# A post-layernorm transformer layer on one core: the output products stand behind the third query-key product, the row maxima go through DRAM in nine transfers, and the prologue is interleaved

## The chip, the cores and the metric

One Trainium2 chip, one of its cores. The metric is device microseconds of one execution of the whole program, the median of three runs.

## The reference

Sixteen sequences of 512 tokens with 256 channels pass through one layer. `x` is float32, shape (16, 512, 256).

```python
qkv = x @ qkv_w + qkv_b                       # 16 heads of 16 channels
local = local_attention(q, k, v)              # each query sees the 128 keys before it
rq = x @ rq_w + rq_b                          # 4 latent heads of 16 channels
rkv = mean_over_8_tokens(x) @ rkv_w + rkv_b   # 64 latent tokens
remote = latent_attention(rq, rk, rv) @ rout_w + rout_b
gate = sigmoid(local @ gl_w + remote @ gr_w)
x = layernorm(x + (gate * local + (1 - gate) * remote) @ out_w + out_b)
h = gelu(ternary_linear(x, w_up))             # 1024 channels; weights become -1, 0, 1
x = layernorm(x + ternary_linear(h, w_down))  # each linear first divides by the row's rms
```

## The kernel before

All instructions are written by hand for each engine, with semaphores between them; no scheduler moves anything. A sequence `i` goes through three phases of steps. Phase **P** makes what the attention needs: the query and key products `QK` to `QK+3` (128 rows each), which are stored as sums of three bf16 parts, the latent attention (`LAT_RQ`, `LAT_RKV`, `LAT_SCORES`, `LAT_EXP`, `LAT_NORM`, `LAT_T`, `LAT_O`, `REMOTE`) and the value products `VALUES` to `VALUES+3`. Phase **A/S/PV** is the local attention: 22 steps `A` find the row maxima of the scores, 16 steps `S` make the transposed scores with the maximum subtracted inside the product (its two bf16 parts are two more rows, `MAXR` and `MAXR+1`, of the stacked queries `Qs`), and 16 steps `PV` weigh the values. Phase **F** is the rest of the layer: `GATE`, `OUT` and `OUT+1` (the output products), `NORM`, `NORM+1` (layernorm and rms), `XN_T`, `XN_HI`, `XN_LO` (transpose and split into two fp16 parts), `UP` to `UP+7` with the down products two steps behind, and `END`.

The first half of body `i` is the local attention of sequence `i` with the maxima of `i+1` between its steps (`order_of_attention`). The second half interleaves phase F of sequence `i` with phase P of sequence `i+2`; its order is the table `SECOND_HALF`, which TensorE, ScalarE, VectorE and GpSimd all walk from top to bottom, each doing its own share of every step. So the table sets the order on all four engines at once, and an engine that waits in one step holds up its share of all the steps below. Fourteen of the sixteen bodies have P steps in their second half. Before body 0 stands the prologue (`order_of_prologue`), which holds phase P of sequences 0 and 1 and the steps A of sequence 0.

A query-key block is split in place. `QK+c` leaves the product in a PSUM bank; ScalarE copies it to `parts[:, 0]` as bf16 (L767); step `SPLIT+2c` subtracts that part in the bank on TensorE (L1392) and ScalarE copies the rest to `parts[:, 1]` (L774); `SPLIT+2c+1` does it again for `parts[:, 2]`. Only after this third copy is the bank given back (`p_taken`, L778). There are four such banks, and phase P hands them out in turn, in the order in which its results stand in the program: a result takes the bank of the result four places before it.

```python
                        act.wait_ge(part2, count(s, 4, t))
                        act.sem_inc(p_taken[bank], 1)
```

Step `LAT_RKV` is one copy `rqT` and four copies `lat_bd` on ScalarE (L783, L790) and then two small operations on VectorE that wait for them (L1076). `LAT_SCORES` on TensorE (L1424) waits for `lat_bd` as well. On ScalarE the feed-forward starts with an ACT_TABLE_LOAD and the GELU (L883), of which the first frees the bank for `UP+2` on TensorE.

SyncE issues all the DMAs in one stream. `restack(i+2)` writes the parts to DRAM (three DMAs for queries, three for keys, each waiting for its parts) and reads them back as stacks `Qs` and `Ks` (six and six). `move_max(i+1)` copies the transposed maxima `nmax_pair` (128 partitions, 2 parts, 64 columns) into the two rows of `Qs`; it waits for `split_maxima` on VectorE, which stands at step `UP+1`. The first step S of a sequence waits for these transfers (L1514).

## Time and profile before

| | |
|---|---|
| median of three runs | 1172.93 us (1171.77 to 1175.84) |
| the profiled execution | 1171.74 us |
| its span, first to last instruction | 1170.0 us |
| TensorE matmul busy | 994.1 us, 85% of the span |
| VectorE, ScalarE, GpSimd busy | 823.3, 741.7, 628.1 us |
| mean granted TensorE clock | 0.96 of 2.4 GHz |

The span has a prologue of 98.0 us up to the first step S, then bodies of about 66.3 us each (the first steps S start at 98.0, 169.2, 235.6, 301.8, 368.2 us and so on), and the last two bodies, which have less beside them. The busy time of a matmul contains waiting in the pipeline, so where TensorE bounds is read from its idle times and what ended them, stage by stage.

### The profile page before, as it was taken

To read this page: it belongs to the slowest core of one execution; us is meant where nothing else is said; L and a number is where in the kernel's file an instruction comes from. 1 tells how busy PE (TensorE), PEld (TensorE's weight loads), DVE (VectorE), ACT (ScalarE), POOL (GpSimd) and SP (SyncE) were. 2 spreads that over 40 slices of the span, in tenths; PEclk is the share of its full clock that TensorE was granted. 3 is DMA by queue.
4 is the path that set the end of the run, shared out by engine and by line. 5 is a ranking of instruction groups with operands and counts; after the bars stand their busy time and mean duration, and the time that the engine had idled before them with its cause. 6 is when DMAs were issued, how large, how long until landed. Compare 5 with 4: busy or idle time off the path is not lost. (4 is left out here: it accounts for less than half of the span.)

```text
span 1170.0 us, 37047 instructions
## 1 busy us (share of the span) xinstructions
PE 994.1 (85%) x15432; PEld 634.8 (54%) x15432; DVE 823.3 (70%) x1781; ACT 741.7 (63%) x1189; POOL 628.1 (54%) x790
## 2 busy tenths in 40 slices
PE   6765999898989989888999889898989988884755
PEld 3444565565656555565656555565656555562433
DVE  4485777786868777686868778686867768684544
ACT  3523666767676676767676677767676676762544
POOL 6014455665746465664746466574745466572754
PEclk8896999999999999999999999999999999996887
DMA  5731331506152341516143240516143250601000
GB/s 192 199 103 57 109 92 48 152 24 182 40 154 66 100 120 48 137 40 181 40 127 93 86 133 28 157 40 180 40 128 92 68 135 10 176 21 38 1 19 19
DMA packets 58868, 107.46 MB, mean 92 GB/s; under 512 B 20518, under 2 KB 38726, under 8 KB 55622
## 3 DMA queue, kind: packets, MB, share of 16 engines
q1 hardware_dynamic: 58556, 105.08, 31.8%
q8 instruction: 122, 2.00, 0.7%
q14 instruction: 46, 0.38, 0.1%
q10 hardware_dynamic: 144, 0.00, 0.0%
HBM read 70.87 MB, written 33.55 MB: 89 GB/s over the span
## 5 line engine op out<-in xcount | busy, mean ns | idle before, releaser
L847 ACT ACTIVATE Pt<-scores 128x1024 f32<-128x1024 f32 (+1 forms) x256 | 229.6, 917 | 143.9 <-PE oacc L1552 82.0
L1125 DVE TENSOR_REDUCE nmax<-work 128x3 f32<-128x480 f32 x352 | 215.1, 633 | 31.5 <-PE work L1503 28.2
L701 POOL TENSOR_TENSOR h_lo<-hbuf,h_hi 128x512 f16<-128x512 f32 x128 | 148.1, 1157 | 139.8 <-DVE h_hi L1252 139.8
L671 POOL TENSOR_SCALAR_AFFINE_SELECT Pt<-Pt 128x512 f32<-128x512 f32 x256 | 164.2, 642 | 67.6 <-ACT Pt L847 67.2
L685 POOL TENSOR_TENSOR rs<-rs,power 128x6 f32<-128x6 f32 x32 | 42.4, 1325 | 247.5 <-DVE rs L1229 247.5
L1552 PE MATMUL oacc<-Pt,Vp 128*32 128x256 f32 (+1 forms) x2048 | 153.2, 360 | 15.2 <-POOL Pt L675 9.4
L1529 PE MATMUL scores<-Qs,Ks 100*32 100x160 bf16 (+4 forms) x4096 | 119.9, 230 | 46.9 <-DMA Qs<-nmax_pair 25.7
L1498 PE MATMUL work<-Ks,Qs 98*32 98x160 bf16 x4096 | 146.3, 236 | 14.5 <-DVE nmax L1125 10.5
L1252 DVE CAST h_hi<-hbuf 128x512 f16<-128x512 f32 x128 | 69.2, 540 | 100.3 <-ACT hbuf L883 99.8
L1529 PEld LDWEIGHTS scores<-Qs,Ks 100*32 100x32 bf16 x4096 | 82.4, 98 | 92.2 <-ACT Pt L847 51.0
L1382 PE MATMUL scores<-xT,wqk 128*128 128x512 f32 x256 | 123.3, 616 | 6.5 <-DMA xT<-x_t 6.5
L1565 PE MATMUL oacc<-wdn_t,h_hi 128*128 128x256 f16 x512 | 118.1, 273 | 9.8 <-POOL h_lo L701 9.8
L675 POOL TENSOR_SCALAR_AFFINE_SELECT Pt<-Pt 128x512 f32<-128x512 f32 x192 | 121.8, 635 | 0.0
L1565 PE MATMUL oacc<-wdn_t,h_lo 128*128 128x256 f16 x512 | 117.9, 273 | 0.0
L774 ACT ACTIVATE parts<-scores,bqk 128x512 bf16<-128x512 f32 x128 | 86.2, 685 | 49.6 <-PE scores L1392 47.3
L883 ACT ACTIVATE hbuf<-work 128x512 f32<-128x512 f32 x128 | 76.0, 594 | 60.9 <-PE work L1622 59.1
L1498 PEld LDWEIGHTS work<-Ks,Qs 98*32 98x32 bf16 x4096 | 90.6, 97 | 40.3 <-DVE nmax L1125 26.1
L1622 PE MATMUL work<-xnT,wup_t 128*128 128x512 f16 x384 | 99.5, 382 | 5.8 <-DVE h_sum L1258 5.5
L1503 PE MATMUL work<-mask_band,identb 128*32 128x192 bf16 (+1 forms) x1408 | 100.4, 248 | 0.8 <-issue 0.8
L1258 DVE TENSOR_TENSOR h_sum<-h_sum,work 128x512 f32<-128x512 f32 x112 | 76.4, 682 | 10.8 <-ACT work L890 10.5
L1382 PEld LDWEIGHTS scores<-xT,wqk 128*128 128x128 f32 x256 | 48.9, 196 | 57.7 <-issue 54.9
L767 ACT ACTIVATE parts<-scores,bqk 128x512 bf16<-128x512 f32 x64 | 43.7, 683 | 55.5 <-PE scores L1382 55.3
(175 smaller groups left out, 1878.5 us busy)
## 6 DMA issues: line engine op xcount, KB each, us to landing
parts_scratch<-parts SPq DMA_DIRECT2D x96, 256.0 KB, 5.1
Qs<-parts_scratch SPq DMA_DIRECT2D x96, 256.0 KB, 5.0
Ks<-parts_scratch SPq DMA_DIRECT2D x96, 256.0 KB, 5.0
xT<-x_t SPq DMA_DIRECT2D x16, 512.0 KB, 4.0
xres<-x SPq DMA_DIRECT2D x16, 512.0 KB, 4.8
y<-nat SPq DMA_DIRECT2D x16, 512.0 KB, 3.0
Qs<-nmax_pair SPq DMA_DIRECT2D x256, 2.0 KB, 1.8
nat<-up_t SPq DMA_DIRECT2D x1, 1024.0 KB, 6.0
```

The source lines that it names most:

```text
L671: ins = pool.affine_select(out=pt[:, :, 0:P], in_=pt[:, :, 0:P], compare_op=ALU.is_gt, fill=0.0, base=0, pattern=[[0, 4], [1, P]], channel ...
L675: ins = pool.affine_select(out=pt[:, :, P:2 * P], in_=pt[:, :, P:2 * P], compare_op=ALU.is_ge, fill=0.0, base=0, pattern=[[0, 4], [-1, P]] ...
L701: pool.tensor_tensor(h_lo[:, t % NR, :], hbuf[:, t % 2, :], h_hi[:, t % NR, :], ALU.subtract).then_inc(h_lo_ready, 1)
L847: nc.scalar.activation(Pt[:, u % NPT, :, 0:w], scores[:, slot, :, :].rearrange("p k (h q) -> p (k h) q", h=2)[:, :, 0:w], ACT.Exp, scale=S ...
L1125: nc.vector.tensor_reduce(nmax[:, first:first + n], work[:, slot, 0:n * BAND].rearrange("p (h c) -> p h c", h=n), X, ALU.max, negate=True) ...
L1382: mm = nc.tensor.matmul(p_bank(bank), wqk[:, t, c * P:(c + 1) * P], xT[:, t, :], start=(t == 0), stop=False, skip_group_check=True)
L1498: nc.tensor.matmul(work[g * GT:(g + 1) * GT, slot, i * BAND:(i + 1) * BAND], q[0:KA, h, at:at + GT], kk[0:KA, h * S + at:h * S + at + BAND ...
L1503: mm = nc.tensor.matmul(o[:, :, 0:NG + 1:NG, :], identb[:, g * GT:(g + 1) * GT], mask_band[:, :, :].unsqueeze(1).to_broadcast([P, n, 2, GT ...
L1529: mm = nc.tensor.matmul(scores[g * GT:(g + 1) * GT, slot, c // 2, (c % 2) * 2 * P + lo:(c % 2) * 2 * P + hi], kk[0:KB, key + lo:key + lo + ...
L1552: mm = nc.tensor.matmul(oacc[c * PVW:(c + 1) * PVW, hg % 2, j * P:j * P + w], Vp[:, s.par, j, h * VW:h * VW + PVW], Pt[:, v % NPT, c, 0:w] ...
L1565: mm = nc.tensor.matmul(oacc[:, b // 2, (b % 2) * D:(b % 2 + 1) * D], (h_hi, h_lo)[j][:, f % NR, b * P:(b + 1) * P], wdn_t[:, f, :], start ...
L1622: mm = nc.tensor.matmul(work[:, slot, :], wup_t[:, t, f * P:(f + 1) * P], xnT[:, part, t, :], start=(part == 0 and t == 0), stop=(part == ...
```

## The change

Three edits.

The table `SECOND_HALF`: `OUT` moves from behind `QK+3` and `SPLIT+3` to directly behind `SPLIT+2`, that is, behind the third product; `OUT+1` follows two subtractions later; `QK+3` comes after it. `NORM` and `NORM+1` now stand ahead of `LAT_RKV`, with `LAT_RQ` and one subtraction between them. `SPLIT+7` comes after `LAT_RKV`; `XN_T` and `XN_T+1` come ahead of `VALUES+1` and `LAT_SCORES`; `LAT_EXP` and `LAT_EXP+1` come after `XN_LO`. From `UP` on the table is as it was.

The maxima: eight DMAs write `nmax_pair` to a scratch tensor in DRAM, in the layout of the two rows; SyncE waits until they have landed; a ninth DMA reads both rows into `Qs`. Before, sixteen DMAs wrote the rows directly.

The prologue: all steps P of sequence 1 stand between the steps A of sequence 0, whereas before its first fourteen stood ahead of them; the sums of the weights' magnitudes (`SUMS`) move from ahead of the first step A to behind the fourteenth.

```diff
--- before.py
+++ after.py
@@ -75,10 +75,10 @@
 END = UP + FT
 SECOND_HALF = (
     ("F", GATE), ("P", QK), ("P", QK + 1), ("P", SPLIT), ("P", QK + 2), ("P", SPLIT + 1), ("P", SPLIT + 2),
-    ("P", QK + 3), ("P", SPLIT + 3), ("F", OUT), ("P", SPLIT + 4), ("P", SPLIT + 6), ("P", LAT_RQ), ("P", SPLIT + 5),
-    ("F", OUT + 1), ("P", SPLIT + 7), ("P", LAT_RKV), ("P", VALUES), ("P", LAT_SCORES), ("F", NORM),
-    ("F", NORM + 1), ("P", LAT_EXP), ("P", VALUES + 1), ("F", XN_T), ("F", XN_T + 1), ("F", XN_HI),
-    ("P", LAT_EXP + 1), ("F", XN_LO), ("P", VALUES + 2), ("F", UP), ("P", LAT_NORM), ("F", UP + 1),
+    ("F", OUT), ("P", SPLIT + 3), ("P", SPLIT + 4), ("F", OUT + 1), ("P", QK + 3), ("P", SPLIT + 5), ("F", NORM),
+    ("P", LAT_RQ), ("P", SPLIT + 6), ("F", NORM + 1), ("P", VALUES), ("P", LAT_RKV), ("P", SPLIT + 7),
+    ("F", XN_T), ("F", XN_T + 1), ("P", VALUES + 1), ("P", LAT_SCORES), ("F", XN_HI), ("F", XN_LO), ("P", LAT_EXP),
+    ("P", LAT_EXP + 1), ("P", VALUES + 2), ("F", UP), ("P", LAT_NORM), ("F", UP + 1),
     ("P", VALUES + 3), ("P", LAT_NORM + 1), ("F", UP + 2), ("F", UP + 3), ("P", LAT_T), ("P", LAT_T + 1),
     ("F", UP + 4), ("P", LAT_O), ("F", UP + 5), ("P", REMOTE), ("F", UP + 6), ("P", REMOTE + 1), ("F", UP + 7),
     ("F", END))
@@ -140,13 +140,15 @@
     order += [("P", 0, k) for k in (LAT_SCORES, LAT_EXP, LAT_EXP + 1, VALUES, VALUES + 1, LAT_NORM, LAT_NORM + 1,
                                     VALUES + 2, VALUES + 3)]
     order += [("P", 0, LAT_T), ("P", 0, LAT_T + 1), ("W", 0, CONSTANTS)]
-    order += [("P", 1, k) for k in split]
-    order += [("P", 0, LAT_O), ("P", 1, LAT_RQ), ("P", 1, LAT_RKV), ("W", 0, SUMS)]
-    between = {1: [("P", 0, REMOTE)], 3: [("P", 0, REMOTE + 1)], 5: [("P", 1, VALUES)], 7: [("P", 1, LAT_SCORES)],
-               9: [("P", 1, LAT_EXP)], 10: [("P", 1, LAT_EXP + 1)], 12: [("P", 1, VALUES + 1)],
-               13: [("P", 1, LAT_NORM), ("P", 1, LAT_NORM + 1)], 14: [("P", 1, VALUES + 2)],
-               16: [("P", 1, LAT_T), ("P", 1, LAT_T + 1)], 17: [("P", 1, VALUES + 3)], 18: [("P", 1, LAT_O)],
-               20: [("P", 1, REMOTE), ("P", 1, REMOTE + 1)]}
+    order.append(("P", 0, LAT_O))
+    after = {0: [(0, REMOTE), (1, QK)], 1: [(1, QK + 1), (1, SPLIT)], 2: [(0, REMOTE + 1)],
+             3: [(1, QK + 2), (1, SPLIT + 1), (1, SPLIT + 2)], 4: [(1, QK + 3), (1, SPLIT + 3)],
+             5: [(1, SPLIT + 4), (1, SPLIT + 6)], 6: [(1, SPLIT + 5), (1, LAT_RQ), (1, SPLIT + 7)], 7: [(1, LAT_RKV)],
+             8: [(1, VALUES)], 9: [(1, LAT_SCORES)], 11: [(1, LAT_EXP)], 12: [(1, LAT_EXP + 1), (1, VALUES + 1)],
+             14: [(1, LAT_NORM), (1, LAT_NORM + 1)], 15: [(1, VALUES + 2)], 17: [(1, LAT_T), (1, LAT_T + 1)],
+             18: [(1, VALUES + 3)], 19: [(1, LAT_O)], 21: [(1, REMOTE), (1, REMOTE + 1)]}
+    between = {v: [("P", i, k) for i, k in steps] for v, steps in after.items()}
+    between[13] = [("W", 0, SUMS)]
     for v in range(NM):
         order.append(("A", 0, v))
         order += between.get(v, [])
@@ -331,6 +333,7 @@
         scores = ctx.enter_context(nc.psum_tensor("scores", [P, 2, 2, 512], F32))
         oacc = ctx.enter_context(nc.psum_tensor("oacc", [P, 2, 512], F32))
 
+        nmax_dram = nc.dram_tensor("nmax_scratch", [2, H * S], BF16, kind="Internal").ap()
         parts_dram = nc.dram_tensor("parts_scratch", [3, 2, P, 2 * S], BF16, kind="Internal").ap()
 
 
@@ -376,6 +379,7 @@
         s_taken = [sem(f"s_taken{k}") for k in range(2)]
         nmax_vec = sem("nmax_vec")
         nmax_split = sem("nmax_split")
+        nmax_out = sem("nmax_out")
         nmax_in = [sem(f"nmax_in{k}") for k in range(2)]
         masked = sem("masked")
         pv_done = sem("pv_done")
@@ -535,14 +539,16 @@
             def move_max(s):
 
                 wait_alone(sp, nmax_split, count(s, 1, 0))
-                for j in range(2):
-                    row = Qs[s.par][MAXR + j:MAXR + j + 1, :, :].rearrange("a h n -> a (h n)").rearrange(
-                        "a (k r w) -> a k r w", k=2, w=P)
-                    for g in range(NG):
-                        quadrant = slice(g * GT, (g + 1) * GT)
-                        for k in range(2):
-                            sp.dma_start(row[:, k, :, quadrant], nmax_pair[quadrant, j, k * GT:(k + 1) * GT]
-                                         ).then_inc(nmax_in[s.par], 16)
+                if not s.first:
+                    wait_alone(sp, nmax_in[1 - s.par], (s.half + s.par) * 16)
+                scratch = nmax_dram.rearrange("j (k r g w) -> g r j k w", k=2, g=NG, w=GT)
+                for g in range(NG):
+                    for j in range(2):
+                        sp.dma_start(scratch[g, :, j], nmax_pair[g * GT:(g + 1) * GT, j, :].rearrange(
+                            "p (k w) -> p k w", k=2)).then_inc(nmax_out, 16)
+                wait_alone(sp, nmax_out, count(s, 1, 0) * 16 * 2 * NG)
+                sp.dma_start(Qs[s.par][MAXR:MAXR + 2, :, :].rearrange("j h n -> j (h n)"), nmax_dram
+                             ).then_inc(nmax_in[s.par], 16)
 
             def store_before(s):
 
@@ -1132,7 +1138,7 @@
                     slot, k = work_use(s, "A", v)
                     dve.wait_ge(w_taken[slot], k + 1)
                 if not s.first:
-                    dve.wait_ge(nmax_in[1 - s.par], (s.half + s.par) * 16 * 4 * NG)
+                    dve.wait_ge(nmax_out, count(s, 1, -1) * 16 * 2 * NG)
                 nc.vector.transpose(nmaxT[:, :], nmax[:, :]).then_inc(nmax_vec, 1)
                 dve.wait_ge(nmax_vec, count(s, 2, 0))
                 nc.vector.tensor_copy(nmax_pair[:, 0, :], nmaxT[:, :]).then_inc(nmax_vec, 1)
@@ -1511,7 +1517,7 @@
                 hg, j = u // NB, u % NB
                 slot, k = score_use(s, u)
                 if u == 0:
-                    pe.wait_ge(nmax_in[s.par], (s.half + 1) * 16 * 4 * NG)
+                    pe.wait_ge(nmax_in[s.par], (s.half + 1) * 16)
                     if s.first:
                         pe.wait_ge(q_consts, 2)
                 if u < 2 and not s.last:
```

The table sets the order on every engine, so its effect is shown as the program of each engine has it. In these rows `scores<-xT,wqk` is a query-key product, `scores<-parts,minusb` a subtraction, `work<-wout,mixT` an output product, `scores<-wv,xT` a value product, `scores<-lat_bd,rqT` the latent scores, `oacc<-ident,mixT` the transposes of `XN_T`, and `oacc<-xnT,minus` the product of `XN_LO`.

TensorE, second half of a body, from the third query-key product on, before:

```order
L1382 MATMUL scores<-xT,wqk 128x512 x2
L1392 MATMUL scores<-parts,minusb 128x512
L1581 MATMUL work<-wout,mixT 128x256 x4
L1584 MATMUL work<-bout_rows,ones_b 128x256 x2
L1392 MATMUL scores<-parts,minusb 128x512 x2
L1399 MATMUL scores<-xT,wrq 64x256 x4
L1392 MATMUL scores<-parts,minusb 128x512
L1581 MATMUL work<-wout,mixT 128x256 x4
L1584 MATMUL work<-bout_rows,ones_b 128x256 x2
L1392 MATMUL scores<-parts,minusb 128x512
L1409 MATMUL scores<-pooled,wrk 64x64 x4
L1413 MATMUL scores<-wrv,pooled 64x64 x4
```

and after:

```order
L1587 MATMUL work<-wout,mixT 128x256 x4
L1590 MATMUL work<-bout_rows,ones_b 128x256 x2
L1398 MATMUL scores<-parts,minusb 128x512 x2
L1587 MATMUL work<-wout,mixT 128x256 x4
L1590 MATMUL work<-bout_rows,ones_b 128x256 x2
L1388 MATMUL scores<-xT,wqk 128x512 x2
L1398 MATMUL scores<-parts,minusb 128x512
L1405 MATMUL scores<-xT,wrq 64x256 x4
L1398 MATMUL scores<-parts,minusb 128x512
L1370 MATMUL scores<-wv,xT 128x272 x2
L1415 MATMUL scores<-pooled,wrk 64x64 x4
L1419 MATMUL scores<-wrv,pooled 64x64 x4
```

The first output product moved ahead of the fourth query-key product, and the latent keys and values moved behind the first value product.

TensorE a little further down, after the change, with the semaphores that it waits for:

```order
L1597 MATMUL oacc<-ident,mixT 128x128
L1597 MATMUL oacc<-ident,mixT 128x128 [waits xn_ready]
L1597 MATMUL oacc<-ident,mixT 128x128
L1370 MATMUL scores<-wv,xT0 128x272 [waits p_taken3]
L1370 MATMUL scores<-wv,xT0 128x272
L1430 MATMUL scores<-lat_bd,rqT 128x256 [waits p_taken0,p_taken1,bd_ready]
L1430 MATMUL scores<-lat_bd,rqT 128x256 x3
```

The second value product now stands behind the transposes and ahead of the latent scores; before, it stood behind the latent scores. Its bank is that of the fourth query-key product (`p_taken3`), where before it was that of the latent keys and values.

ScalarE, second half, from the third query-key copy on (`parts<-scores,bqk` are the copies of the split, `mixT<-ytok,nbias,rs` those of `NORM`, `Vp<-scores` those of the values), before:

```order
L767 ACTIVATE parts<-scores,bqk 128x512
L774 ACTIVATE parts<-scores,bqk 128x512 x5
L783 ACTIVATE rqT<-scores,brq 128x256
L790 ACTIVATE lat_bd<-scores,lat_fold 128x64 x4
L806 ACTIVATE Vp<-scores 128x16x17
L864 ACTIVATE mixT<-ytok,nbias,rs 128x256 x4
L799 ACTIVATE Pt<-Pt 128x512
L806 ACTIVATE Vp<-scores 128x16x17
L870 ACTIVATE xnT<-oacc 128x512 x2
L799 ACTIVATE Pt<-Pt 128x512
L874 ACTIVATE xnT<-oacc 128x512 x2
L806 ACTIVATE Vp<-scores 128x16x17
```

and after:

```order
L773 ACTIVATE parts<-scores,bqk 128x512
L780 ACTIVATE parts<-scores,bqk 128x512
L870 ACTIVATE mixT<-ytok,nbias,rs 128x256 x2
L780 ACTIVATE parts<-scores,bqk 128x512
L870 ACTIVATE mixT<-ytok,nbias,rs 128x256 x2
L812 ACTIVATE Vp<-scores 128x16x17
L789 ACTIVATE rqT<-scores,brq 128x256
L796 ACTIVATE lat_bd<-scores,lat_fold 128x64 x4
L780 ACTIVATE parts<-scores,bqk 128x512
L812 ACTIVATE Vp<-scores 128x16x17
L876 ACTIVATE xnT<-oacc 128x512 x2
L880 ACTIVATE xnT<-oacc 128x512 x2
```

The last copy of the split moved from ahead of `rqT` and `lat_bd` to behind them, and the exponentials of the latent scores (`Pt<-Pt`) moved behind the copies of `XN_HI` and `XN_LO`.

TensorE in the prologue, behind the gate's bias, after the change (`work<-Ks,Qs` is a step A of sequence 0; before, the first of them stood behind all the query-key products and subtractions of sequence 1):

```order
L1673 MATMUL oacc<-gcol,bog 128x1 x2
L1466 MATMUL scores<-Pt,rv_bd 32x256 x4
L1504 MATMUL work<-Ks,Qs 32x160 x12
L1509 MATMUL work<-mask_band,identb 32x3x2x32 x4
L1476 MATMUL scores<-lat_oT,wro 128x256 x4
L1388 MATMUL scores<-xT,wqk 128x512 x2
L1504 MATMUL work<-Ks,Qs 32x160 x12
L1509 MATMUL work<-mask_band,identb 32x3x2x32 x4
L1388 MATMUL scores<-xT,wqk 128x512 x2
L1398 MATMUL scores<-parts,minusb 128x512
L1504 MATMUL work<-Ks,Qs 32x160 x12
L1509 MATMUL work<-mask_band,identb 32x3x2x32 x4
```

The first step A has only one small product ahead of it here, and the query-key products of sequence 1 follow it.

## Rows read from the trace of the kernel before

**Rows 1.** Who waited for whom, TensorE, 107 to 1050 us: total, times, longest
```profile
PE oacc L1599 <- ACT xnT L870: 12.9, 14, 1.0
PE scores L1424 <- ACT lat_bd L790: 12.4, 14, 1.1
```

**Rows 2.** Timeline of TensorE in body 3: start us, us, instruction, idle before it
```profile
323.16 3.70 PE L1382 MATMUL scores<-xT,wqk 128*128 128x512 f32 x8
...
331.38 1.89 PE L1581 MATMUL work<-wout,mixT 128*128 128x256 f32 x8
...
333.32 0.59 PE L1392 MATMUL scores<-parts,minusb 128*128 128x512 bf16 x2
...
345.32 1.08 PE L1364 MATMUL scores<-wv,xT 128*128 128x272 f32 x4
346.24 1.89 PE L1611 MATMUL work<-xnT,wup_t 128*128 128x512 f16 x8
...
348.88 1.03 PE L1622 MATMUL work<-xnT,wup_t 128*128 128x512 f16 x4
```

**Rows 3.** Timeline of VectorE in the same body
```profile
328.59 0.71 DVE L1209 STREAM_TRANSPOSE mixT<-x 128x512 f32<-128x512 f32 x1
...
331.24 0.71 DVE L1209 STREAM_TRANSPOSE mixT<-x 128x512 f32<-128x512 f32 x1
```

**Rows 4.** Timeline of GpSimd in the same body
```profile
335.64 1.32 POOL L685 TENSOR_TENSOR rs<-rs,power 128x6 f32<-128x6 f32 x1 [12.89 <-DVE rs L1229]
```

**Rows 5.** Timeline of ScalarE in the same body
```profile
337.45 0.69 ACT L774 ACTIVATE parts<-scores,bqk 128x512 bf16<-128x512 f32 x1 [1.47 <-PE scores L1392]
...
338.63 1.28 ACT L790 ACTIVATE lat_bd<-scores,lat_fold 128x64 f32<-128x64 f32 x4
339.79 0.42 ACT L806 ACTIVATE Vp<-scores 128x272 f32<-128x272 f32 x1
341.09 2.08 ACT L864 ACTIVATE mixT<-ytok,nbias,rs 128x256 f32<-128x256 f32 x4 [0.89 <-DVE nbias L1239]
343.15 0.63 ACT L799 ACTIVATE Pt<-Pt 128x512 f32<-128x512 f32 x1
...
345.44 1.09 ACT L874 ACTIVATE xnT<-oacc 128x512 f16<-128x512 f32 x2
...
346.85 1.28 ACT L883 ACT_TABLE_LOAD   x1
348.15 0.60 ACT L883 ACTIVATE hbuf<-work 128x512 f32<-128x512 f32 x1
```

**Rows 6.** Timeline of TensorE in the prologue
```profile
38.62 5.36 PE L1382 MATMUL scores<-xT,wqk 128*128 128x512 f32 x8
...
56.13 0.39 PE L1498 MATMUL work<-Ks,Qs 98*32 98x160 bf16 x12
...
98.03 1.26 PE L1529 MATMUL scores<-Qs,Ks 100*32 100x160 bf16 x32 [14.55 <-DMA Qs<-nmax_pair]
```

**Rows 7.** Timeline of SyncE's DMA issues, prologue and body 3
```profile
40.27 3.65 SPq L532 DMA_DIRECT2D Ks<-parts_scratch  x6
...
86.78 10.02 SPq L544 DMA_DIRECT2D Qs<-nmax_pair  x16
...
346.83 3.65 SPq L532 DMA_DIRECT2D Ks<-parts_scratch  x6
352.93 10.46 SPq L544 DMA_DIRECT2D Qs<-nmax_pair  x16
```

**Rows 8.** From issue to landing, all DMAs of L532
```profile
DMA to landing us min/median/max: 3.2/5.0/6.8
```

**Rows 9.** The same for the DMAs of L525
```profile
DMA to landing us min/median/max: 2.0/5.1/9.5
```

**Rows 10.** Stretches: length, busy time by engine, granted TensorE clock, DMA share, GB/s
```profile
62.50:69.30 6.80, 4.83 (x120) 3.02 (x122) 5.28 (x10) 1.03 (x2) 0.28 (x1) 1.00 0.68 204
69.30:72.70 3.40, 3.40 (x44) 2.18 (x44) 2.26 (x4) 1.03 (x2) 2.21 (x2) 0.50 1.01 231
```

## The prediction

> **What bounds the kernel now.** I read the waits of TensorE over the fourteen bodies that have P steps first. Outside the attention two of them come back in every body: the product of `XN_LO` waits 0.9 us for ScalarE's `xnT`, and the latent scores wait 0.9 us for ScalarE's `lat_bd` [rows 1]. Then the timelines of one second half, body 3, taken as typical since these waits have the same count as the bodies. Let t = 0 be 323.16, where TensorE leaves the attention for `QK`. `UP+2` starts at t = 25.72 [rows 2]. It stands behind the first GELU, which runs from t = 24.99 [rows 5] and frees its bank 0.6 us later, so the engine to follow up to this point is ScalarE: its chain of copies decides when the feed-forward starts, and everything behind that (GELU, `h_hi`, `h_lo`, down product) hangs on it in an order that the change leaves alone. What the new table is worth is the new start of the first GELU, times 14. Lastly the prologue, where TensorE stands still 14.55 us for the maxima [rows 6] while SyncE issues sixteen DMAs [rows 7].
>
> **Part 1, the table, walked through.** The chain on VectorE up to `mixT` isn't touched: its transposes end at t = 6.14 and 8.79 [rows 3]. TensorE: two products take 3.70 [rows 2], the third half as much, so with three subtractions of some 0.2 it is done at 6.0. `OUT` takes 1.94, from its start to the subtraction behind it [rows 2]; it now starts at 6.2 instead of 8.2 and ends at 8.1. Two subtractions of about 0.2 follow, then `OUT+1` waits until 8.8 for the second `mixT` and ends at 10.8. The fourth product, 1.7 behind that, is complete at 12.5 and its copy starts at 12.7. Before, this copy ran at about 7.8. That is the first cost: ScalarE, done with the third product's copies at about 10, stands idle until 12.7.
>
> The statistics do come earlier. The first rstd ended 5.58 after the start of `OUT` (336.96 against 331.38) [rows 2, 4], so now at 11.8, and the second at about 14.4; the copies of `NORM`, which before started at t = 17.93 [rows 5], since VectorE had to do `LAT_RKV` first, can start at 14.0, as soon as ScalarE has done the two split copies.
>
> From 12.7 on ScalarE has this left before the GELU: four split copies at 0.69, four copies of `NORM` 2.08, three value copies at 0.42, `rqT` of about the same 0.4, `lat_bd` 1.28, two exponentials at 0.63, `XN_HI` and `XN_LO` 1.09 each, the table load 1.30 [rows 5]. Sum 12.5. Neighbours overlap by about 0.1 (`lat_bd` 338.63, next start 339.79, 1.16 for its 1.28), so 11.7 at the least. Even if ScalarE never waited again, the GELU would start at 24.4 to 25.2, against 24.99 now. **The table can hardly win anything**: the bound is -0.6 us a body.
>
> But it does wait, at places that the new order makes. ScalarE in a row: third-part copy until 14.0, two of `NORM` until 15.0, split copy 15.6, two of `NORM` 16.6, value 17.0, `rqT` 17.3, `lat_bd` 18.5, last split copy 19.3. TensorE in the meantime has done `XN_T` by 17.3 and stands at `VALUES+1`, whose bank is that of the fourth product, given back only by that last copy. So it waits 2.0 us, and multiplies from 19.3 to 20.2 (0.92, the distance from the start of one to the start behind it, 345.32 to 346.24, and 0.1 of drain) [rows 2]. ScalarE has the copy of `VALUES+1` ahead of `XN_HI`: it waits too, 1.1 us, and copies at 20.4. `XN_HI` is then 20.7 to 21.75, `XN_LO` has to wait for TensorE's product until 22.2 and ends at 23.2. The latent scores start at 20.2, are there at 21.6, and VectorE's four operations of 0.7 release the exponentials at 23.2 and 24.5 (0.6 idle). The last value copy ends at 25.3, the table load at 26.6. **GELU at 26.6 instead of 24.7**, where the same way of stepping through the old order gives 24.7 for the 24.99 of the trace. So +1.9 us a body; the waits make it up (1.1 + 0.5 + 0.7, less the 0.4 that the bound leaves). Fourteen bodies: **+26.9 us**. What lies behind the GELU moves with it. Both ends: -0.6 x 14 = -8 if no wait arises, and +3 x 14 = +42 if the latent scores' exponentials come a further 1.1 late, the size of ScalarE's wait for `VALUES+1`.
>
> **The transfers beside it** don't decide. The last part of the keys is ready at t = 19.4 instead of 15.0 (337.45 + 0.69) [rows 5]; before, the reads of the stack began only at 23.7 [rows 7], behind the transfers of the queries. A DMA of this line lands 2.0 at best and 5.1 in the median [rows 9]: the reads start between 23.7 and 24.6 and are down by about 33. The maxima go out at 29.77 in the trace [rows 7] and now at 31.7, take some 9.7 (below), and are wanted by the next body at 45.0 + 1.9. That leaves 5 us of cover; if it were gone, each body would pay the excess. SyncE's loads of `xT` and `xres` behind it come 1.5 us sooner, with nobody waiting.
>
> **Part 2, the maxima.** Sixteen issues and a landing are 11.25 us (86.78 to 98.03) [rows 6, 7], 0.63 an issue. Eight issues put the last one 4.4 after the first. What follows isn't in this trace. Landing in DRAM is bounded by 2.0 and 5.1 [rows 9]; I take 2.0, since nothing is queued ahead. The ninth reads 16 KB into one partition each, as a row of a stack does; its landing is bounded by 3.2 and 5.0 [rows 8]; I take 3.2 for the same reason. Sum 9.7 with 0.1 for SyncE's wait: 1.5 less, bounds 3 less (two bare landings of 2) and 3.3 more. TensorE feels it at two places only, ahead of body 0 and ahead of the last sequence, the others being hidden. **-3 us**, from -6 to +7.
>
> The Trainium skill, "DMA: Bandwidth & Descriptors", Rules for kernel authors, says that a DMA whose outermost dimension is smaller than 16 is confined to that many engines. The ninth has two rows; by that rule it moves on two engines, which agrees with taking the row of a stack for it, and were it spread instead, the sum would be about 1 us less at each of the two places.
>
> **Part 3, the prologue.** TensorE started the steps A at 56.13, behind 17.5 us of sequence 1's products [rows 6]. Now it stands at the first step A after some 1.1 us of them (`LAT_O`) and waits for the keys of sequence 0, whose last read is issued at 43.3 and lands 5.0 to 6.8 later [rows 7, 8], at 48.3 to 50.1; I take 49.7, 6.4 earlier than before. The other 16.4 us come in between the steps. Unhidden that is +10.0. In their waits for VectorE the steps A of the prologue hide some of it; the old stretch of 27 us had some 6 us, so +4 is the best. On the other hand TensorE has now stood idle for 10 us, after which the trace shows it at 1.2 GHz; two products took 5.36 at 38.62 against 3.70 at the full clock [rows 2, 6]. I take **+6**, bounds 0 and +12.
>
> **Sum.** 1171.7 + 26.9 - 3 + 6 = 1201.6 for an execution like the profiled one, whose span is 1170.0; the median of the runs shown is 1.2 above it: 1203.
>
> **Rival 1: the clock.** The table makes two waits of TensorE, 2.0 us at `VALUES+1` and 1.5 us at `UP+2`, where it had none over 1.0. In the prologue a stretch with 2 us idle of 6.8 was followed by one at half the clock, 1.2 GHz [rows 10]. If that comes in the bodies, the products behind it take what they took at 38.62: 1.66 us more for two, some 1.7 us a body, 24 us in all: 1227. Against it: ScalarE, not TensorE, ends the chain there, which hides a part. The Trainium skill, "TensorE: Matmul & The Clock Gate", A second HAM failure mode, describes just this, pauses between PSUM banks that make the clock swing between its two levels; rows 10 agree that a pause of this size can do it.
>
> **Rival 2, the other side: the waits are filled.** If the last split copy comes before `XN_T` is done (decided by whether ScalarE has it out by t = 17.3, not 19.3), `VALUES+1` doesn't wait, the GELU starts at its bound of 24.4, and each body gains up to 0.6: -8 - 3 + 2 gives 1164. For it speaks that the statistics come 3.9 us earlier; against it, the 11.7 us of copies that stand behind the fourth product whatever happens.
>
> **Rival 3: absorbed.** TensorE waits for `h_lo` and for the squares later in every body; should the shift vanish there, only prologue and maxima stay: 1176. The first GELU heads all of that, so I believe it little.
>
> **Chances.** Forecast (1190 to 1213) 0.63, clock (1213 to 1235) 0.2, absorbed (1170 to 1184) 0.07, filled (1155 to 1169) 0.1. The range 1184 to 1230 holds eight in ten. A measurement of this kernel tells about 0.3% (3.5 us) from no change. Faster by more than that 0.1, within it 0.04, slower 0.86.
>
> **What would show it.** In a body after: `OUT` at t = 6.2, the fourth product's copy at 12.7, TensorE idle about 2 us ahead of the second value product with ScalarE's L780 as releaser, the GELU at 26.6, bodies of 68.2 us instead of 66.3. In the prologue: the first step A near 49.7, the first step S near 102. DMAs: eight issues and a ninth in about 9.7. I am wrong if the bodies are no longer than 66.3 us, if `VALUES+1` doesn't wait, or if the granted clock falls inside the bodies.

## The result, and the profile after

The changed kernel takes 1204.18 us (median of 4 runs, 1201.17 to 1210.66), the kernel before beside it on the same chip 1172.48 us (1171.77 to 1175.84). The ratio is 1.027, 95% interval 1.023 to 1.032. The profiled execution took 1204.33 us against 1171.77, which is 32.6 more, and its span is 1202.6 us.

From the page of the kernel after: span, busy time by engine, granted clock in tenths, two groups of instructions with the idle time ahead of them, and the new transfers with their median landing:

```profile
span 1202.6 us, 36968 instructions
PE 1009.0 (84%) x15432; PEld 635.4 (53%) x15432; DVE 820.4 (68%) x1781; ACT 743.3 (62%) x1189; POOL 628.2 (52%) x790
PEclk8787999999999999999999999999999999997877
L773 ACT ACTIVATE parts<-scores,bqk 128x512 bf16<-128x512 f32 x64 | 43.8, 685 | 109.5 <-PE scores L1388 109.4
L1370 PE MATMUL scores<-wv,xT 128*128 128x272 f32 x256 | 74.3, 417 | 28.0 <-ACTq L784 28.0
nmax_scratch<-nmax_pair SPq DMA_DIRECT2D x128, 4.0 KB, 1.5
```

The busy times show no culprit. The idle time does: TensorE now stands 28.0 us ahead of value products. The waits of TensorE from 107 to 1100 us (total, times, longest), which answer to [rows 1]:

```profile
PE scores L1370 <- ACTq L784: 28.0, 14, 2.0
PE work L1628 <- ACT hbuf L889: 19.1, 14, 1.5
```

Both come once in each of the fourteen bodies. The two waits of [rows 1] are gone; the new ones are twice and one and a half times as long.

Body 3 on TensorE, which answers to [rows 2]. TensorE leaves the attention at 334.71, which is t = 0:

```profile
334.71 3.70 PE L1388 MATMUL scores<-xT,wqk 128*128 128x512 f32 x8
...
340.91 1.99 PE L1587 MATMUL work<-wout,mixT 128*128 128x256 f32 x8
...
345.61 1.88 PE L1388 MATMUL scores<-xT,wqk 128*128 128x512 f32 x4
...
354.11 1.18 PE L1370 MATMUL scores<-wv,xT 128*128 128x272 f32 x4 [2.00 <-ACTq L784]
...
362.37 1.04 PE L1628 MATMUL work<-xnT,wup_t 128*128 128x512 f16 x4 [1.48 <-ACT hbuf L889]
```

`OUT` starts at t = 6.2, the fourth query-key product at 10.9, and `VALUES+1` waits 2.00 us until 19.4. ScalarE in the same body, which answers to [rows 5]:

```profile
343.37 1.49 ACT L780 ACTIVATE parts<-scores,bqk 128x512 bf16<-128x512 f32 x2 [0.73 <-PE scores L1398]
...
347.52 0.69 ACT L773 ACTIVATE parts<-scores,bqk 128x512 bf16<-128x512 f32 x1 [2.66 <-PE scores L1388]
...
352.15 1.28 ACT L796 ACTIVATE lat_bd<-scores,lat_fold 128x64 f32<-128x64 f32 x4
353.31 0.71 ACT L780 ACTIVATE parts<-scores,bqk 128x512 bf16<-128x512 f32 x1
355.33 0.40 ACT L812 ACTIVATE Vp<-scores 128x272 f32<-128x272 f32 x1 [1.32 <-PE scores L1370]
...
357.15 1.08 ACT L880 ACTIVATE xnT<-oacc 128x512 f16<-128x512 f32 x2 [0.45 <-PE oacc L1605]
...
359.49 0.63 ACT L805 ACTIVATE Pt<-Pt 128x512 f32<-128x512 f32 x1 [0.69 <-DVE Pt L1094]
...
361.72 0.60 ACT L889 ACTIVATE hbuf<-work 128x512 f32<-128x512 f32 x1
```

ScalarE idles 2.66 us until the fourth product's copy at t = 12.8. Its last split copy (353.31) stands behind `lat_bd`, and gives back the bank for which `VALUES+1` waits. Then ScalarE waits for that product itself, for `XN_LO`'s product, and for VectorE: 1.32 + 0.45 + 0.69. The first GELU starts at t = 27.0; before it was 24.99. Measured from the end of the last attention product instead, it starts at 26.94 in every undisturbed body after, and at 24.91 or 24.92 in most bodies before: 2.03 us later, and the next attention starts 2.03 later too (46.97 against 44.94). Nothing between absorbs it.

The maxima through DRAM, SyncE's timeline in the prologue; with it the landing times of all the writes of L547 in the run, and TensorE's first step S:

```profile
94.16 3.62 SPq L547 DMA_DIRECT2D nmax_scratch<-nmax_pair  x8
98.91 0.24 SPq L550 DMA_DIRECT2D Qs<-nmax_scratch  x1
...
DMA to landing us min/median/max: 1.4/1.5/3.5
...
101.76 1.26 PE L1535 MATMUL scores<-Qs,Ks 100*32 100x160 bf16 x32 [11.13 <-DMA Qs<-nmax_scratch]
```

From the first issue to the step S it is 7.6 us, where it was 11.25 [rows 6, 7].

Where the 32.6 us are, by the starts of the steps S in the two traces: the first one comes 3.8 later (101.8 against 98.0), the fourteen bodies take 33.4 more (967.1 against 933.7), the stretch from there to the first step S of the last sequence 4.2 less (28.98 against 33.16), the next one 1.1 less, and the tail 0.7 more. Of the 33.4, 14 x 2.03 = 28.4 is the later GELU. The rest is something the bodies of before never had: between 107 and 1055 us before, TensorE's granted clock is never below 1.00. After, it falls to 1.2 GHz in bodies 0, 1, 4, 11 and 13. In bodies 0, 4, 11 and 13 it falls at the wait ahead of `VALUES+1` or within 1.5 us behind it; in body 1, and a second time in body 0, it falls behind the wait ahead of `UP+2`. In body 11, three stretches in order of time (length; busy us and instructions of PE, PEld, DVE, ACT, POOL; granted clock; DMA share; GB/s), and the product that starts as the clock falls:

```profile
898.60:902.00 3.40, 1.43 (x11) 0.94 (x9) 0.38 (x2) 3.40 (x10) 3.40 (x3) 1.00 0.96 231
902.00:905.40 3.40, 3.24 (x10) 2.14 (x12) 0.00 (x0) 1.08 (x4) 2.60 (x3) 0.50 0.64 227
905.40:908.80 3.40, 3.40 (x22) 2.04 (x19) 2.44 (x4) 2.00 (x4) 0.00 (x0) 1.00 0.70 174
...
902.16 2.18 PE L1370 MATMUL scores<-wv,xT 128*128 128x272 f32 x4 [2.00 <-ACTq L784]
```

The value product that took 1.18 in body 3 takes 2.18 here, and the GELU starts at 28.47 instead of 26.94. In the five bodies with such a stretch the next attention starts 2.1, 0.6, 1.1, 1.5 and 0.9 us later than 2.03 would have it, 6.2 together. Three bodies of before were 0.6 late in sum themselves, and the attentions were 0.7 shorter: 28.4 + 6.2 - 0.6 - 0.7 = 33.3 of the 33.4.

### The profile page after: what moved, and what is told of

Read it like the earlier page. It is cut to its first block and busy times, and to the rows that moved or that the text cites. A ratio compares the mean times of both kernels' runs of the same rounds, so it can differ in the third digit from the quotient of the medians.

```text
span 1202.6 us, 36968 instructions
## 1 busy us (share of the span) xinstructions
PE 1009.0 (84%) x15432; PEld 635.4 (53%) x15432; DVE 820.4 (68%) x1781; ACT 743.3 (62%) x1189; POOL 628.2 (52%) x790
## 5 line engine op out<-in xcount | busy, mean ns | idle before, releaser
L1628 PE MATMUL work<-xnT,wup_t 128*128 128x512 f16 x384 | 101.1, 386 | 24.1 <-ACT hbuf L889 19.3
L1370 PE MATMUL scores<-wv,xT 128*128 128x272 f32 x256 | 74.3, 417 | 28.0 <-ACTq L784 28.0
```

The source lines that it names most:

```text
L1628: mm = nc.tensor.matmul(work[:, slot, :], wup_t[:, t, f * P:(f + 1) * P], xnT[:, part, t, :], start=(part == 0 and t == 0), stop=(part == ...
```

## The experiments

Each group ran on one chip with its own runs of the kernel before, whose medians were 1169.44 (9 runs), 1174.36 (7) and 1170.11 (7). Differences are taken within a group. "GELU at" is always counted from the end of the last attention product of the body, in an undisturbed body, one without a fall of the clock (24.92 before, 26.94 after).

### The three parts alone

**table_only** has the new `SECOND_HALF` and nothing else of the change.

> The kernel before with the new second-half table and nothing else of the change. Theory (ScalarE's chain to the first GELU): the first GELU moves from t = 24.9 to 26.9 behind the end of the attention, as it stands in the changed kernel, so each of the fourteen bodies is 2.0 us longer: 1172.5 + 28 = 1201, and up to 1206 if stretches at 1.2 GHz come with it. Rival (the table is neutral and prologue and maxima carry the loss): within 4 us of 1172.5.

Measured: 1205.34 us (1202.56 to 1213.70), ratio 1.033 (1.029 to 1.037), +35.9. GELU at 26.94, and the waits of TensorE in its bodies are those of after:

```profile
PE scores L1365 <- ACTq L779: 28.1, 14, 2.0
PE work L1623 <- ACT hbuf L884: 20.0, 14, 1.5
```

The whole loss is in the table, as expected. Its granted clock fell in four bodies (0, 3, 7, 8), at a price of 4.9 us.

**maxima_only** has the nine transfers and nothing else.

> The kernel before with the nine transfers of the maxima through DRAM and nothing else. Theory: TensorE feels the maxima at two places alone. Its waits there were 14.5 and 11.2 us and are 11.1 and 7.3 us in the changed kernel, so this gives 3.4 + 3.9 = 7 us: 1165. Rival (the transfers through DRAM also delay something in the bodies, where their 5 us of cover is thin): no gain or a loss, 1172 or more.

Measured: 1161.34 us (1160.52 to 1165.28), ratio 0.993 (0.991 to 0.996), -8.1, 3.7 below the 1165 expected. The bodies are unchanged (GELU at 24.93). The gain is at the two places where TensorE stands and waits for the maxima: the first step S comes 5.1 earlier (3.7 of it from the chain, which takes 7.6 us instead of 11.25, the rest because the maxima were ready 1.4 earlier in this trace), and the part behind the fourteen bodies is 3.6 shorter.

**prologue_only** has the interleaved prologue and nothing else.

> The kernel before with the interleaved prologue and nothing else. Theory: TensorE stands at the first step A for the keys of sequence 0 (12 us in the changed kernel), and the work moved behind it isn't hidden: the first step S comes some 7 us later (101.8 against 98.0 with 3.4 us gained by the maxima), so 1179 to 1181. Rival (the interleaving gains and the later start comes from elsewhere): 1172 or less.

Measured: 1173.89 us (6 runs, 1171.12 to 1177.32), ratio 1.004 (1.002 to 1.006), +4.5. TensorE stands 11.94 us for the keys ahead of the first step A at 49.75, and the first step S comes 3.5 later than before. The expectation of 1179 to 1181 was too high by 5 us: it took its 7 us from a trace in which the clock fell in the prologue, as the next run shows.

**after_again** is the changed kernel once more, in the second group.

> The changed kernel itself, to stand beside the next three on one chip. 1204 as measured, or 1201 if this chip runs the kernel before in 1169.5 as the last one did.

Measured: 1204.79 us (1203.89 to 1209.33), ratio 1.027 (1.022 to 1.031); GELU at 26.95. This second trace has its first step S at 98.2, not 101.8, and shows why. The stretch from 79 to 86 us, first of after, then of after_again (columns as above):

```profile
79.00:86.00 7.00, 6.24 (x72) 4.15 (x76) 5.15 (x9) 5.29 (x9) 0.41 (x1) 0.53 0.72 181
...
79.00:86.00 7.00, 4.98 (x96) 3.27 (x98) 5.25 (x9) 5.07 (x8) 0.41 (x1) 1.00 0.79 187
```

The same place at a granted clock of 0.53 did 72 products in 6.24 busy us, and at 1.00 it did 96 in 4.98. Between these two traces the first step S differs by 3.6 us. The other traces with this prologue agree. Where the clock stays up around 80 us, SyncE issues the maxima at 89.8, 90.2 and 90.3 (fourth_early, after_again, prologue_only); behind a fall of 6.8 us it issues them at 94.0 and 94.2 (v1_late, after), behind one of 3.4 us at 90.9 (last_split_early). In the seven traces with the old prologue the issue comes at 83.7 to 86.8. So the order of the interleaved prologue costs some 5 us, and a fall of the clock in it nearly as much again.

### What makes the wait at the second value product

**last_split_early**: the changed kernel, with the last split copy ahead of the latent keys and values.

```diff
-    ... ("F", NORM + 1), ("P", VALUES), ("P", LAT_RKV), ("P", SPLIT + 7),
+    ... ("F", NORM + 1), ("P", VALUES), ("P", SPLIT + 7), ("P", LAT_RKV),
```

> The changed kernel with the last subtraction, SPLIT+7, moved from behind LAT_RKV to ahead of it, so that ScalarE gives the bank of VALUES+1 back before it makes rqT and lat_bd. Theory: the wait of TensorE at VALUES+1 (2.0 us a body) falls to 0.6 or less, and ScalarE's wait for that product with it; the latent scores still wait for lat_bd. The GELU starts 0.7 us earlier, 26.2, so 10 us over fourteen bodies: 1194, and 2 to 4 less if the stretches at 1.2 GHz vanish too. Rival (the bank is only where a shortage of ScalarE shows; its copies behind the fourth product bound the body whatever their order): 1204, unchanged.

Measured: 1184.96 us (1182.83 to 1187.13), ratio 1.013 (1.011 to 1.016), where the changed kernel has 1.027: some 16 us less, and 9 below the 1194 expected. GELU at 26.06. Waits of TensorE in the bodies, then ScalarE's last split copy in body 3, whose t = 0 is 325.1:

```profile
PE work L1629 <- ACT hbuf L890: 20.7, 14, 1.5
...
342.10 0.68 ACT L781 ACTIVATE parts<-scores,bqk 128x512 bf16<-128x512 f32 x1
```

The copy runs at t = 17.0 instead of 18.6, the 2.0 us wait is gone, and with it 0.88 us a body, 12.3 in all. The clock still falls in seven bodies, but late and cheaply (0.6 to 0.8 us each), since the wait ahead of `UP+2` is left. The other rival, that ScalarE's copies bound the body whatever their order, is out.

**fourth_early**: the changed kernel, with the fourth product back ahead of `OUT`, all behind it as the change has it.

```diff
-    ("F", OUT), ("P", SPLIT + 3), ("P", SPLIT + 4), ("F", OUT + 1), ("P", QK + 3), ("P", SPLIT + 5), ...
+    ("P", QK + 3), ("F", OUT), ("P", SPLIT + 3), ("P", SPLIT + 4), ("F", OUT + 1), ("P", SPLIT + 5), ...
```

> The changed kernel with the fourth query-key product back ahead of OUT; all the rest of the new table stays. Theory (what costs is the order behind the output products, the bank wait and ScalarE's queue, not the late fourth product): ScalarE's waits behind it stay, OUT and all behind it come later by 1.7 less what the waits swallow, and stepping through the order gives the first GELU at 27.3 on the scale on which the changed kernel's was 26.6: 0.6 us a body later, 1212. Rival (the late fourth product is the loss, since ScalarE stood idle for it from t = 10 to 12.7): 1.9 us a body faster, 1178.

Measured: 1223.64 us (1219.25 to 1232.75), ratio 1.042 (1.037 to 1.048), 18.9 above after_again and 12 above the 1212 expected. Waits of TensorE in the bodies:

```profile
PE scores L1371 <- ACTq L785: 28.1, 14, 2.0
PE scores L1399 <- ACT parts L781: 16.8, 14, 1.2
PE work L1629 <- ACT hbuf L890: 16.4, 14, 1.5
```

The bank wait is 2.0 us to the digit although the product is now early. What it waits for is the last split copy, and that stands in ScalarE's queue behind the four copies of `NORM`, `rqT` and `lat_bd`, wherever the product is. So the lateness of the fourth product isn't the cause of this wait; the place of its copies is. `OUT` now starts 1.4 later (7.55), the statistics with it, and the split copies queued behind `NORM` too. The one body without a fall of the clock has its GELU at 27.36, 0.4 later than after. The other thirteen are at 28.1 to 29.5, all with a stretch at 1.2 GHz. Three waits in place of two, and the clock falls in nearly every body: I had priced the waits and not the clock.

**v1_late**: the changed kernel, with `VALUES+1` behind `XN_LO` and the latent scores directly behind the transposes.

```diff
-    ("F", XN_T + 1), ("P", VALUES + 1), ("P", LAT_SCORES), ("F", XN_HI), ("F", XN_LO), ("P", LAT_EXP),
+    ("F", XN_T + 1), ("P", LAT_SCORES), ("F", XN_HI), ("F", XN_LO), ("P", VALUES + 1), ("P", LAT_EXP),
```

> The changed kernel with VALUES+1 moved from behind XN_T+1 to behind XN_LO; the last split copy stays where it is. Theory (the wait for the bank costs because ScalarE's copy of this product stands ahead of XN_HI): XN_HI starts 1.4 us earlier, VALUES+1 finds its bank free, the latent scores wait for lat_bd instead. Stepping through gives the GELU 0.9 us earlier, 26.0 behind the attention, 13 us over fourteen bodies, and some of the stretches at 1.2 GHz go as well: 1186 to 1192. Rival (any order behind the late fourth product ends at the same time): 1204.

Measured: 1198.05 us (1193.15 to 1201.65), ratio 1.022 (1.018 to 1.026). That is above the 1186 to 1192 expected, though a part of the expectation held: the GELU is at 26.05 in two bodies. In the other twelve it is at 27.2 or 27.3, each with its stretch at 1.2 GHz. Waits of TensorE in the bodies, then two stretches of body 2:

```profile
PE scores L1431 <- ACTq L785: 30.9, 14, 2.2
...
281.50:284.90 3.40, 1.20 (x8) 0.78 (x7) 0.38 (x2) 3.28 (x10) 3.40 (x4) 1.00 0.92 246
284.90:288.30 3.40, 3.34 (x14) 2.08 (x15) 0.68 (x1) 0.97 (x2) 2.31 (x2) 0.50 0.75 275
```

The wait didn't go, it moved to the latent scores and grew to 2.2 us. L785 is the line that gives back the bank behind the last split copy, so what is waited for is the same copy. The low stretches start at 216.6, 284.9, 353.2, 421.4, 489.7: 68.3 us apart, where these bodies are 68.3 to 69.5 us long, and each starts 19 to 20 us behind the end of its attention. Bodies 8 and 9, with the same wait, have no such stretch. Why a body has one or not, no run here shows.

### What the late fourth product costs by itself

**out_early** is the kernel before with `OUT` and `OUT+1` ahead of the fourth product, and the order behind it as before.

```diff
-    ("P", QK + 3), ("P", SPLIT + 3), ("F", OUT), ("P", SPLIT + 4), ("P", SPLIT + 6), ("P", LAT_RQ), ("P", SPLIT + 5),
-    ("F", OUT + 1), ("P", SPLIT + 7), ("P", LAT_RKV), ("P", VALUES), ("P", LAT_SCORES), ("F", NORM), ...
+    ("F", OUT), ("P", SPLIT + 3), ("P", SPLIT + 4), ("F", OUT + 1), ("P", QK + 3), ("P", SPLIT + 5),
+    ("P", SPLIT + 6), ("P", LAT_RQ), ("P", SPLIT + 7), ("P", LAT_RKV), ("P", VALUES), ("P", LAT_SCORES), ...
```

> The kernel before (its maxima and its prologue) with the output products moved to where the changed kernel has them, behind the third query-key product, and the rest of the table in its old order; SPLIT+5 and SPLIT+6 follow the late fourth product ahead of LAT_RQ. Theory (a late fourth product alone delays the last split copy, lat_bd and all behind by 1.1 us, since the statistics, which come earlier, wait behind LAT_RKV on VectorE as before): first GELU 1.1 us later, 26.0 after the attention, 16 us over fourteen bodies: 1188. Rival (output products that start 2 us earlier shorten the chain): 1172 or less.

Measured: 1204.09 us (1202.22 to 1207.96), ratio 1.025 (1.021 to 1.029): a miss by 16 us. GELU at 27.07, not 26.0. Two operations of VectorE in body 4, and the one of GpSimd beside them:

```profile
416.48 0.16 DVE L1240 SCALAR_TENSOR_TENSOR nbias<-mv,rs 128x2 f32<-128x2 f32 x1
...
416.95 1.22 DVE L1240 SCALAR_TENSOR_TENSOR nbias<-mv,rs 128x2 f32<-128x2 f32 x1
...
416.88 2.50 POOL L731 TENSOR_TENSOR rem<-rem,rem_b 128x512 f32<-128x512 f32 x2
```

The same operation on 128x2 takes 0.16 us, and 1.22 when it is issued 0.07 after GpSimd's first bias addition; 2.50 for two is 1.25 each, so it ends with the first. ScalarE waits for it, and so does the rest of the body. Body 0, in which GpSimd has no bias addition at this place, has its GELU at 26.16.

**bias_first** is out_early with GpSimd's two bias additions ahead of its four `x1` operations instead of behind them.

```diff
+                    if s.next().exists and not s.first:
+                        bias_remote(s.next())
                     for b in range(NB):
...
-                    if s.next().exists and not s.first:
-                        bias_remote(s.next())
```

> The kernel of out_early, with GpSimd adding the bias of the remote part (two additions of 1.26 us) ahead of the four operations that make x1, instead of behind them. In out_early VectorE's last nbias, an operation on two elements of 0.16 us elsewhere, took 1.22 us, and it began while the first of these additions ran. Theory (VectorE was held up by that addition): the operation is back at 0.16 to 0.25 us, the first GELU comes 1.0 us earlier, at 26.0 behind the attention instead of 27.1, and fourteen bodies give 14 us: 1190 where out_early had 1204. Rival (the 1.22 us belongs to the operation or its waits): 1204, unchanged.

Measured: 1187.97 us (1187.49 to 1192.49), ratio 1.015 (1.012 to 1.019). That is 16.1 us below out_early, and 11.5 by the two ratios, since before ran 4 us faster in this group; the two spans differ by 15.0 (1201.2 and 1186.2). GELU at 26.15, the operation is back at 0.16, and no body has a stretch at 1.2 GHz. The same operation in body 4:

```profile
412.32 0.16 DVE L1240 SCALAR_TENSOR_TENSOR nbias<-mv,rs 128x2 f32<-128x2 f32 x1
```

So the collision cost 0.92 us in thirteen bodies, 12.0, and out_early's falls of the clock in three bodies another 3.6, against the 15.0 between the spans; in the old order the late fourth product by itself costs 26.15 - 24.92 = 1.23 us a body, 17.2 in all, against the 17.9 measured. The Trainium skill, "SBUF — State Buffer", section Who interferes with whom, says that only the pair of ports shared by VectorE and GpSimd causes contention, as an exclusive lock, and that a VectorE instruction with two SBUF inputs contends with a GpSimd instruction that reads SBUF. The trace agrees: `nbias<-mv,rs` has two such inputs, and it ends within 0.05 us of the first addition. I hadn't looked for it in a step this small.

### The same idle time filled

**new_table** keeps `OUT` early and the fourth product late, but moves `LAT_RQ` and `LAT_RKV` ahead of it, so that ScalarE has `rqT` and `lat_bd` to do while it waits. `VALUES` comes late, where TensorE is free. The maxima go through DRAM, the prologue is the old one.

```diff
-    ("F", OUT), ("P", SPLIT + 3), ("P", SPLIT + 4), ("F", OUT + 1), ("P", QK + 3), ("P", SPLIT + 5), ("F", NORM),
-    ("P", LAT_RQ), ("P", SPLIT + 6), ("F", NORM + 1), ("P", VALUES), ("P", LAT_RKV), ("P", SPLIT + 7),
-    ("F", XN_T), ("F", XN_T + 1), ("P", VALUES + 1), ("P", LAT_SCORES), ("F", XN_HI), ("F", XN_LO), ("P", LAT_EXP),
-    ("P", LAT_EXP + 1), ("P", VALUES + 2), ("F", UP), ...
+    ("P", LAT_RQ), ("F", OUT), ("P", SPLIT + 3), ("P", SPLIT + 4), ("F", OUT + 1), ("P", LAT_RKV),
+    ("P", SPLIT + 5), ("P", QK + 3), ("P", LAT_SCORES), ("F", NORM), ("F", NORM + 1), ("P", SPLIT + 6),
+    ("F", XN_T), ("F", XN_T + 1), ("P", LAT_EXP), ("F", XN_HI), ("P", SPLIT + 7), ("P", LAT_EXP + 1),
+    ("P", VALUES), ("F", XN_LO), ("P", VALUES + 1), ("P", VALUES + 2), ("F", UP), ...
```

> Old prologue, maxima through DRAM in nine transfers, and a third order of the second half, found by stepping through the order with the durations of the trace: OUT stays behind the third product, LAT_RQ goes ahead of it and LAT_RKV behind OUT+1, so that ScalarE makes rqT and lat_bd while it would wait for the fourth product; the latent scores come ahead of NORM, the first value product only behind XN_HI. Theory: ScalarE's idle time between the third product's copies and the fourth's is filled, the GELU starts at 23.3 on the scale on which before is 24.7, UP+2 1.6 us earlier, 22 us over fourteen bodies, and 7 to 8 us from the maxima: 1143. Rival (the earlier start is given back in the up and down products, which are bound by other waits): 1165, what the maxima alone give.

Measured: 1144.19 us (1138.58 to 1147.03), ratio 0.973 (0.969 to 0.978), faster than both kernels. ScalarE in body 3, with t = 0 at 309.8:

```profile
319.22 1.49 ACT L779 ACTIVATE parts<-scores,bqk 128x512 bf16<-128x512 f32 x2 [1.54 <-PE scores L1397]
...
322.00 1.29 ACT L795 ACTIVATE lat_bd<-scores,lat_fold 128x64 f32<-128x64 f32 x4 [0.93 <-PE scores L1418]
...
324.03 0.69 ACT L772 ACTIVATE parts<-scores,bqk 128x512 bf16<-128x512 f32 x1 [0.16 <-PE scores L1387]
...
333.26 0.60 ACT L888 ACTIVATE hbuf<-work 128x512 f32<-128x512 f32 x1
```

The fourth copy comes even later than in after (t = 14.2 against 12.8), but ScalarE waits 0.16 us for it and not 2.66, and from it to the GELU it is 9.2 us instead of 14.2. GELU at 23.45, 1.5 us a body earlier than before. The idle stretch itself is filled only in part: from the third product's copies up to and with the fourth's, ScalarE waits 1.54 + 0.93 + 0.16 = 2.63 us here and 0.73 + 2.66 = 3.39 in after. The waits behind it, 0.18 + 1.32 + 0.45 + 0.69 = 2.64 us in after, are gone altogether. Together ScalarE waits 3.4 us less than in after, and the GELU comes 3.49 earlier. Which of the moves (`lat_bd` ahead of the product, the latent scores ahead of `NORM`, the value products late) removed the waits behind, no run parts. No wait of TensorE in a body is over 0.83 us, and the clock stays at 2.4 GHz from 99 us to the end of the fourteenth body.

**new_table_again** is the same kernel in the third group.

> The kernel of new_table again, on the same chip as the third prologue: 1144, 0.973 of the kernel before.

Measured: 1143.23 us (1135.83 to 1144.85), ratio 0.975 (0.971 to 0.979).

**third_prologue** adds to new_table a middle way in the prologue: three of sequence 1's query-key products ahead of the first step A, the fourth and the rest between the steps.

```diff
+    order.append(("P", 0, LAT_O))
+    order += [("P", 1, k) for k in (QK, QK + 1, SPLIT, QK + 2, SPLIT + 1, SPLIT + 2, SPLIT + 3)]
+    after = {0: [(0, REMOTE)], 1: [(1, QK + 3)], 2: [(1, SPLIT + 4), (1, SPLIT + 6), (1, SPLIT + 5)],
+             3: [(0, REMOTE + 1)], 4: [(1, LAT_RQ), (1, SPLIT + 7)], 5: [(1, LAT_RKV)], 6: [(1, VALUES)],
...
```

> The kernel of new_table with a third prologue: sequence 1's first three query-key products and four of its subtractions stand ahead of the first step A, in the time in which TensorE would wait for the keys of sequence 0, and the rest between the steps A, the remote products ahead of the last one. Theory (the changed prologue lost its 4 to 5 us to this wait of 12 us with nothing in it): the wait is 3 to 5 us, the first step S comes 3 us earlier than in new_table, 1141. Rival (VectorE's maxima bound the stretch whatever fills it): 1144, unchanged or worse.

Measured: 1145.55 us (1138.53 to 1147.10), ratio 0.977 (0.973 to 0.981), the same as new_table_again beside it. TensorE at the first step A of third_prologue, then the stretch from it to the issue of the maxima, in third_prologue and in new_table:

```profile
50.85 0.59 PE L1505 MATMUL work<-Ks,Qs 98*32 98x160 bf16 x12 [1.89 <-DMA Ks<-parts_scratch]
...
50.90:88.30 37.40, 29.68 (x439) 17.21 (x440) 24.20 (x43) 13.85 (x25) 5.94 (x8) 0.84 0.44 129
...
54.00:83.70 29.70, 21.53 (x408) 13.45 (x406) 23.92 (x43) 10.13 (x19) 5.38 (x5) 0.93 0.53 135
```

The wait for the keys fell to 1.89 us, and the steps start 3 us earlier, yet take 7.7 longer. So the first step S comes 5.2 us later (96.4 against 91.2), where 3 earlier was expected. Its fourteen bodies took 4.3 us less than those of new_table_again (911.6 against 915.9), all of it in the attentions, so that the spans differ by 1.3 us only (1143.4 against 1142.1). VectorE has the same work in both (24.2 and 23.9 us), so it doesn't set this. TensorE is busy 8 us more, at a lower granted clock (0.84 against 0.93). What is put between the steps of the prologue isn't hidden: the stretch is longer by about as much as TensorE is busy longer. How much of the 8 us is the clock and how much the moved products, these rows don't part.

## Why the prediction came out

The time was right (1203 forecast, 1204 measured), and so was the mechanism of the table, walked through engine by engine. That the total came within 1.2 us is luck: the table cost 6.5 us more than its term, the maxima gave 4.5 more than theirs, and the clock, left out of the sum, fell inside the bodies, which the prediction itself had named as a sign of being wrong.

- **The table, +26.9 forecast.** Walked through correctly. Nearly every point of the walk has its row: `OUT` at 6.2, the copy at 12.8 (12.7), the wait of 2.00 (2.0) until 19.4 (19.3), ScalarE's waits of 1.32, 0.45 and 0.69 (1.1, 0.5, 0.7), `UP+2`'s wait of 1.48 (1.5). The GELU moved by 2.03, where I had 1.9. fourth_early and last_split_early show the cause of the bank wait to be the queue position of the last split copy, as the walk had it. The 2.03 can't be split into shares. Removing the bank wait gave 0.88 back. The late product costs 1.23 in the old order (bias_first), but in the new order taking it away made the GELU 0.4 later (fourth_early).
- **Rival 1, the clock, came in beside the forecast.** I had made it a separate case of 24 us, all bodies or none. What happened is a part of it: in the profiled execution it came in five bodies of fourteen, 6.2 us, and in that of after_again in eight, some 10 us. So the table cost 33 to 37 (33.4 over the fourteen bodies of after, 36.6 over those of after_again, table_only +35.9) and not 27. The step that failed is treating the clock as one event with a chance of 0.2, and so putting it at nothing in the sum; it is an event in each body. In v1_late and fourth_early it came in twelve and thirteen bodies and cost some 14 and 19 us. The price of 1.7 us a body was near the upper end of what a fall cost in after (0.6 to 2.1). The prediction also says that TensorE had no wait over 1.0; [rows 1] has 1.1; and the 2 us idle in the stretch of [rows 10] were several pauses, the longest 1.42 us, so those rows don't show what a single pause of 2.0 does. The Trainium skill, "TensorE: Matmul & The Clock Gate", A second HAM failure mode, describes a kernel that cycles through PSUM banks and leaves TensorE idle for moments so often that the clock swings between its two levels. The trace agrees in part: in after the clock fell at the pause of 2.00 us ahead of `VALUES+1` in four bodies and behind the one of 1.48 ahead of `UP+2` in two, while nine bodies with the same pauses stayed at 2.4 GHz.
- **The maxima, -3 forecast, about -7.5 measured** (7.6 us for the chain where I had 9.7, so 3.7 less at each of two places and not 1.5; -8.1 alone). All three prices were too high: the issues are 0.45 us apart, not 0.63 (the sixteen old ones wrote into a single partition each; whether that is why, no run shows); the writes land in 1.5, not 2.0; the ninth is 2.9 from issue to step S, not 3.2. The best bound of the range, -6, was passed too: a bare landing is 1.4 at best here, where the row I had used as the lowest says 2.0 [rows 9]. The old transfers of the maxima themselves would have been the nearer row: in the trace of before they land 1.7 us after their issue at best and 1.8 in the median. On how many engines the ninth moved, no run here shows.
- **The prologue, +6 forecast.** +4.5 alone, and +3.8 or +7.4 in the two traces of the changed kernel (first step S 0.2 or 3.8 later than before, and 3.6 added for the shorter chain of the maxima), by whether the clock falls near 80 us. Without that fall the changed kernel's first step S is at 98.2 and not near 102 as forecast. The prediction's bounds don't fit its own text: it calls +4 the best and then puts the lower bound at 0. The first step A came at 49.6 (49.7). That nothing hides the work between the steps was right in kind; third_prologue, built on the opposite hope, gained nothing.
- **Rival 2, the waits filled**, fell for this change, but its idea is what new_table does. Its price was wrong: I bounded the gain at 0.6 us a body because 11.7 us of ScalarE's copies stand behind the fourth product "whatever happens". That holds only for this order. new_table puts `rqT` and `lat_bd` ahead of that copy and gains 1.5. The sum of this rival, 1164, also has +2 for the prologue where the forecast has +6.
- **Rival 3, absorbed**, fell. The next attention moves by the same 2.03 as the GELU.
- **The transfers beside it** indeed don't decide: none of TensorE's waits inside the fourteen bodies is for `Ks`, `Qs` or the maxima.

The sum: table 33.4 (6.5 more than forecast), prologue and maxima ahead of body 0 +3.8 (forecast +4.5), maxima at the second place -4.2 (forecast -1.5), the last sequence and the tail -0.4. Together 32.6 against 29.9.
